# A graph network on one core: VectorE widens tiles ahead of ending early sums and of copying a normed group back

## The reference

```python
x = layernorm(x + gcn_block(x))     # two GCN layers, a gate and a bias
x = layernorm(x + rgcn_block(x))    # two relational layers, 8 relations

def gcn_conv(x, src, dst, W, b):    # with self-loops
    h = x @ W
    norm = dinv[s] * dinv[d]        # dinv = rsqrt(degree)
    return segment_sum(h[s] * norm[:, None], d) + b
```

## Time and profile before

| what | value |
|---|---|
| median of 3 executions | 1518.98 us |
| their spread | 1516.81 to 1519.71 us |
| the profiled execution's own time | 1522.39 us |
| its span | 1520.2 us |
| mean granted clock of PE in it | 0.974 of full speed |
| busy in the span: PE, DVE, ACT, POOL | 90%, 66%, 58%, 56% |

### The profile page before, as it was taken

How to read it: one execution, slowest core, us unless ns; L and a number is a source line. 1 busy time by engine, 2 the same in 40 slices (tenths; PEclk the granted TensorE clock), 3 DMA queues, 4 the chain that set the end, 5 groups by cost and what they waited for, 6 DMA issues and landing times.

```text
span 1520.2 us, 24977 instructions
## 1 busy us (share of the span) xinstructions
PE 1366.5 (90%) x8581; PEld 1077.5 (71%) x8581; DVE 1009.5 (66%) x2376; ACT 885.0 (58%) x1730; POOL 852.5 (56%) x836
## 2 busy tenths in 40 slices
PE   1368887999869999999999999998999999999996
PEld 1356566776527777777778777775878888888885
DVE  8989996666657877867877878864444444444342
ACT  0248873554337776767876777664555555555351
POOL 6710000000037777777777777773777776777574
PEclk9999996999989999999999999999999999999898
DMA  5202111124243443444444444333444444545331
GB/s 135 67 34 88 45 82 60 35 96 165 111 181 115 151 151 115 151 143 162 152 139 144 160 166 151 115 92 135 154 158 152 172 150 141 183 141 182 111 118 41
DMA packets 66774, 191.76 MB, mean 126 GB/s; under 512 B 18756, under 2 KB 24622, under 8 KB 65236
## 3 DMA queue, kind: packets, MB, share of 16 engines
q1 hardware_dynamic: 32788, 93.45, 16.8%
q0 software_dynamic: 26368, 54.05, 13.0%
q10 hardware_dynamic: 7488, 42.60, 7.0%
HBM read 109.38 MB, written 80.65 MB: 125 GB/s over the span
## 4 chain that ended last, share of the span: by engine, by line
PE 74%; DVE 14%; POOL 4%; DMA 3%; issue 3%; ACT 1%; POOLq 0%; DVEq 0%; ACTq 0%
PE ps L1586 12%; PE ps L1587 10%; PE ps L1605 9%; PE ps L1501 9%; DVE hot_mem L1867 9%; PE ps L1572 8%; PE ps L1573 8%; PE ps L1383 3%; PE ps L1384 3%; PE ps L1644 3%; PE ps L1510 3%; PE ps L1630 3%; POOL node_id L947 2%; DMA node_id<-table_rel,edges 2%; DMA acc<-table_rel,edges 1%
## 5 line engine op out<-in xcount | busy, mean ns | idle before, releaser
L947 POOL DMA_INDIRECT node_id<-table_rel,edges x394 | 400.7, 1017 | 496.7 <-DMA table_rel<-node_id 342.7
L947 POOL DMA_INDIRECT acc<-table_rel,edges x384 | 389.1, 1013 | 122.4 <-issue 83.5
L2003 DVE TENSOR_TENSOR hot_mem<-each_h,rel_cols 128x256 f16<-128x256 f16 (+1 forms) x896 | 339.9, 427 | 93.0 <-PE ps L1501 91.2
L1095 ACT ACTIVATE blocks<-ps 128x400 uint16<-128x400 f32 x448 | 224.2, 502 | 133.8 <-PE ps L1501 130.0
L1572 PE MATMUL ps<-wide,high 128*128 128x512 f32 x550 | 289.2, 526 | 0.1
L1501 PE MATMUL ps<-hot_mem 128*128 128x400 f16 x896 | 233.4, 341 | 2.2 <-DVE hot_mem L2003 2.0
L1202 ACT ACTIVATE wide<-blocks 128x512 fp32r<-128x512 uint8 x367 | 225.3, 625 | 0.0
L1573 PE MATMUL ps<-wide,low 128*128 128x512 f32 x550 | 217.3, 395 | 0.0
L1605 PEld LDWEIGHTS ps<-blocks,node_id 128*128 128x128 f32 x878 | 159.0, 191 | 65.3 <-issue 32.1
L1605 PEld LDWEIGHTS ps<-blocks,acc 128*128 128x128 f32 x858 | 157.4, 193 | 43.5 <-issue 9.1
L1867 DVE TENSOR_TENSOR hot_mem<-each_h,edges 128x2048 f16<-128x2048 f16 x200 | 163.6, 890 | 1.2 <-PE ps L1315 0.9
(11 more groups left out here) (208 smaller groups left out, 2247.8 us busy)
## 6 DMA issues: line engine op xcount, KB each, us to landing
rcounts<-blocks ACTq DMA_DIRECT2D x52, 800.0 KB, 3.6
blocks<-rcounts SPq DMA_DIRECT2D x52, 800.0 KB, 4.6
table_rel<-node_id SPq DMA_DIRECT2D x50, 256.0 KB, 2.1
table_rel<-xn SPq DMA_DIRECT2D x50, 256.0 KB
counts<-blocks SPq DMA_DIRECT2D x6, 1600.0 KB, 5.5
blocks<-counts SPq DMA_DIRECT2D x5, 1600.0 KB, 6.9
node_id<-table_rel,edges POOLq DMA_INDIRECT x394
acc<-table_rel,edges POOLq DMA_INDIRECT x384
```

The lines of the kernel that those rows point to most:

```text
L947: nc.gpsimd.indirect_dma_start(got[m % GATHERS][:, j, :], None, tables_rel[layer - 2], bass.IndirectOffsetOnAxis(ap=row_i[:, first + j:fir ...
L1095: nc.scalar.activation(to, ps[:, strip_bank(k), 0:RCELLS].rearrange("p (m t) -> p t m", t=TILES), ACT.Copy, scale=ABOVE)\
L2003: last = nc.vector.tensor_tensor(hot[:, u, :, :], each_h[:, 0:n, :], rel_cols[:, a, first:first + 2].unsqueeze(1).to_broadcast([P, n, 2]), ...
```

## The change

It adds a constant and two calls of `widen1_until` on DVE. The instructions are the same ones in the same number; DVE's order changes, and with it which wait stands ahead of which work.

```diff
+EARLY_ENDS = (8, 8, 10, 12)

                 def gcn_layers():
                     dve.wait_ge(base_ready, 1)
-                    for i in range(EARLY_SUMS):
+                    for i, widened_ in enumerate(EARLY_ENDS):
+                        widen1_until(units_until[EARLY_SUMS] + widened_)
                         end_early(i)
...
                         if 1 <= s < XG:
                             norm_group(s - 1)
+                            widen1_until(units_until[NBLK + s + 1] + LEAD1 + 6)
                         if 2 <= s <= XG + 1:
                             copy_group_back(s - 2)
                             low_part_of(2 * XG + s - 2)
```

## The result

The changed kernel took 1507.17 us in the median of 15 executions (1503.6 to 1517.93), the kernel before 1517.82 us in 15 (1513.04 to 1521.25). The ratio is 0.9939, 95% interval 0.9921 to 0.9956: the change makes it 9.3 us faster by this ratio, between 6.7 and 12.0 (the two medians themselves lie 10.7 us apart). The forecast was 1507.7 us, 11.3 us less than before. The profiled execution took 1507.36 us.

The account below looks back on a forecast made before the run. PE was taken as the bound, with DVE in its place only where PE waits for widening. The gains 6.64 + 1.20 + 1.20 + 0.74 + 1.56 = 11.3 us off 1518.98 gave 1507.7 us, range 1504.5 to 1512.

Parts of the forecast that it names:

- Part one: Early sums: DVE widens units before ending these sums, so PE's stall in sum 4 goes whole, 6.64 us.
- What is late next: After the early sums' reordering: ends 0 and 1 ready 5.6 us before the features read them, so late ending costs nothing.
- Part two: Second layer: three units widened ahead of copy back and low part; gains 1.20, 1.20 and 0.74 us, plus 1.56 of clock.
- Step 1: Second layer, no copy back there: nothing changes and PE's 1.52 us stop stays.
- The new wait: Second layer: the last of three widenings needs four units of the next sum summed; claimed met before DVE arrives.
- steps 2, 3 and 4: Second layer, sums 10, 11, 12: stalls shrink to 0.18 us, about 1.3 us and none.
- the fall in sum 11: PE's clock drop to 0.50 after the 2.47 us stop; claimed gone with a 1.3 us stall, 1.56 us won.
- the rise after sum 4: PE's clock rise claimed to move with the features, costing nothing; bounds: 0.9 us saved, or 1.6 us lost if it misses them.
- rival one: Clock fall in sum 11 stays or rise after sum 4 is late: 1509.3 us with one, 1510.8 with both; chance 0.28.
- rival two: Clock rises early in sum 4: gain 17.6 us, time 1501.4 us; chance 0.05.
- The third: PE's clock stays at 1.2 GHz past the features in sums 5 and 6: costs 20 us, time 1527.7; chance 0.03.
- The fourth: Nothing changes, since PE waits for the counts copy or ACT, not DVE's order: 1519.0 us; chance 0.02.

Follow-up runs that it names:

- e1: Changed kernel without the second widening call, so only the widening ahead of the early sums' ends is kept; 1508.98 us, ratio 0.9951 to the kernel before.
- e4: Changed kernel with the widening ahead of the copy back left out for sum 11 alone; one execution, 1519.1 us.
- e5: Changed kernel with four extra DVE operations ahead of the first early sum's end, DVE 1.0 us later; one execution, 1507.85 us.
- e6: Changed kernel with fourteen extra DVE operations ahead of the first early sum's end, DVE 3.6 us later; one execution, 1511.96 us.
- e8: Changed kernel with DVE and ACT widening 12 units instead of 8 into the next sum ahead of norming a group; 1507.41 us, ratio 0.9917 to before.
- e9: Changed kernel with DVE copying edge numbers and subtracting low parts before ending early sums 2, 3 and 4; 1508.06 us, ratio 0.9933 to before.
- e3: The changed kernel itself, unaltered, measured again in a second set on one chip; 1505.07 us, ratio 0.9911 to the kernel before.
- e7: Changed kernel with eight useless 512-column matmuls on PE while it waits for the last copy of counts; 1507.75 us, ratio 0.9932 to before.
- e10: Changed kernel with DVE's edge copies before early sums 2 to 4 end, plus sixteen useless PE matmuls around the last counts; 1495.42 us, ratio 0.9853 to before.

## Why the prediction was right

**Part one.** The sum gave 6.64 us, the features came 6.85 us sooner. The step held as argued: the hold-up was DVE's order, DVE stood at the last copy of counts (1.34 us, not 1.9) and unit 101 was there in time. The 0.2 us over are the first matmuls of unit 100, which still ran at full clock in this execution (0.30 us and not 0.45); another 0.3 us came at the rise after the features. That is a matter of the execution: e1, e4, e5, e6, e8 and e9 reach the features after 12.35 or 12.36 us, which makes the 6.6 us of the sum, and e3 after 11.80.

**What is late next.** This was the weak step. The prediction named 5.6 us of slack up to the features and said that only the edge copies stand behind the end of sum 4. That is so, but they are the nearer reader: 1.62 us of idle time on DVE ahead of them in the kernel after, up to 2.5 us where the clock rose later. At the forecast's own numbers it cost nothing, so the sum was right; the cover "if PE came 5.7 us earlier it would be gone" should have read 1.6 to 2.5 us. e6 showed it, and e7 paid for it with 4.0 us.

**Part two.** 1.19, 2.80 and 0.73 us against 1.20, 2.76 and 0.74. The stops left over were forecast at 0.2 and 1.3 us and are 0.17 and 1.21. Step 1 kept its 1.52 us. The new wait, four units of the next sum, never held DVE: in steps 2, 3 and 4 it goes from the three widenings to the copy (324.68, 345.91, 366.08) without a gap.

**The clock.** That the fall in sum 11 goes with the stop's length was taken from two stops without a fall; thirteen profiles bear it out. That the rise after sum 4 follows the features held in the profiled execution: it came at about 245, 2.6 us after they began. That it costs nothing is partly luck. With the same work on PE up to that point, the rise came 3.3 to 3.8 us after the start of the features in e1, e3, e5, e6 and e9, 5.2 us in e8, and 8.7 us in e4, where the first 3.7 us of sum 5 ran at half clock:

```profile
246.62 0.78 PE L1384 MATMUL ps<-wide,high 128*128 128x512 f32 x1
247.19 0.63 PE L1385 MATMUL ps<-wide,low 128*128 128x512 f32 x1
...
250.18 0.46 PE L1384 MATMUL ps<-wide,high 128*128 128x512 f32 x1
```

This is the low bound that the prediction gave, the rise that misses the features. In e4 sum 5 ended 2.1 us later than in e5.

**The rivals.** The fall in sum 11 didn't stay, in any kernel with the second part whole. The late rise, the other half of rival one, didn't come in the profiled execution but did in e4, so its 0.28 was not too much. The early rise (rival two) did not come: PE ran from 231.50 to beyond 242 without a pause at 0.50 of full speed. The third would have needed sums 5 and 6 to be slow; they were at 1.00. The fourth fell with the 6.85 us.

**The sum to the time.** It was 11.3 us. The stretch gives 11.85, the first ratio 9.3 (6.7 to 12.0), the second 13.5 us of 1516.94 (10.9 to 16.1). Both intervals hold the forecast.

## What to carry to other kernels

Order an in-order engine's work by when each result is first read, and find the nearest reader behind the moved work, not the one that is named first: here it stood 1.6 us away and not 5.6. Count, for each stop of PE that an edit shortens, whether the granted clock falls after it, since here a stop of 2.4 us cost 1.5 us more than itself and one of 1.3 us did not. Where an early gain is swallowed whole, look which engine became the late one: eight extra matmuls (e7) and DVE's new order (e9) were worth nothing each, and the new order with sixteen of them 6.4 us.

## What the runs showed of the hardware that had not been expected

**Sum 4 ran at either level.** In the changed kernel sum 4's matmuls of 128 columns ran back to back at a granted clock of 0.50, 0.21 us apart, for 11 us with its own part. In e10 the same matmuls ran at 1.00, 0.11 us apart, from the first to the last. In none of the ten profiles without extra matmuls did the clock rise during sum 4; the earliest rise came 2.6 us into the features. In e7 it rose at the end of eight matmuls of 512 columns, 3.4 us. That is one execution, and the rows don't tell what in the work decides it. The Trainium skill, TensorE: Matmul & The Clock Gate, in its part on the clock gate, says that sustained matmul activity releases the throttle; 11 us of back-to-back matmuls in sum 4 did not.

**The clock goes with the spread.** With the same instructions, the part behind the first gather took between 1071.1 us (e1) and 1082.7 us (e4). The profile of before was at a clock of 0.50 from about 1424 to 1438 us, with PE busy all along. The same 60 us in the kernel before and in the kernel after:

```profile
1400.00:1460.00 60.00, 58.96 (x304) 50.77 (x303) 23.91 (x63) 28.04 (x51) 39.19 (x39) 0.89 0.40 133
```

```profile
1400.00:1460.00 60.00, 58.96 (x337) 50.66 (x336) 28.19 (x76) 31.42 (x57) 43.63 (x44) 1.00 0.43 137
```

PE is busy for 58.96 us in both and does 304 matmuls in one and 337 in the other. The busy share doesn't tell the two apart, only the clock does. Over the 15 executions of the changed kernel the mean granted clock went with the time: 0.983 at 1503.6 and 1504.37 us, 0.973 at 1516.29 and 1517.93 us. This is as large as the change itself, and it is why a change of this size was measured by the stretch as well as by the median. What sets off the fall near 1420 us, which e4, e7 and e8 show as well, was not tried.
